# A decoder layer on one core: four edits at the two ends of its attention phase

## The reference, cut to what matters

```python
x = _layernorm(x + attn(x))        # 16 heads of 64, causal, softmax, output projection
x = _layernorm(x + xattn(x, ctx))  # 16 heads of 16, mask by key, biases
x = _layernorm(x + ffn(x))         # two groups of 32 experts, the best 2 of each

def _moe_group(x2, router_w, wg, wu, wd, top_k):
    scores = softmax(x2 @ router_w)
    expert_weights, expert_indices = top_k(scores, 2)
    # tokens sorted by expert, then per expert:
    ys = (silu(xs @ wg[e]) * (xs @ wu[e])) @ wd[e]
    return zeros_like(x2).at[tok].add(ys * weight)
out = (out0 * 2 + out1 * 2) / 4
```

## Time and profile before

| | us |
|---|---|
| median of 3 runs | 4497.11 |
| lowest, highest run | 4495.11, 4508.62 |
| the profiled execution, whole time | 4491.85 |
| its span, first to last instruction | 4490.1 |
| TensorE busy | 4356.7 (97%) |
| VectorE busy | 3698.2 (82%) |
| ScalarE busy | 3259.8 (73%) |
| GpSimd busy | 2742.9 (61%) |

### The profile page before, as it was taken

The page is one execution under the profiler, slowest core; times in us unless marked ns, Lnnn a source line. Parts: engine busy times, 40 slices in busy tenths (PEclk is TensorE's granted clock), DMA queues, the critical chain, the costliest instruction groups (busy, mean ns, idle before and its releaser), DMA issues. The chain is left out here.

```text
span 4490.1 us, 137989 instructions
## 1 busy us (share of the span) xinstructions
PE 4356.7 (97%) x42944; PEld 3811.3 (85%) x42944; DVE 3698.2 (82%) x18057; ACT 3259.8 (73%) x12741; POOL 2742.9 (61%) x3747
## 2 busy tenths in 40 slices
PE   7999999999999999999999999999995999999998
PEld 6988888888888888888888888888883778878886
DVE  4888888888888888888888888888886466658888
ACT  5888888888888888888888888888883444444444
POOL 3466666666666666666656666666566555557777
PEclk9999999999999999999999999999997999999999
DMA  5122121211221212112112111222215699988999
GB/s 170 48 71 67 67 69 65 66 65 63 73 67 65 69 65 66 65 64 73 66 66 68 65 66 65 66 71 67 68 60 162 203 342 342 318 279 284 310 307 290
DMA packets 477453, 552.60 MB, mean 123 GB/s; under 512 B 55632, under 2 KB 408144, under 8 KB 476240
## 3 DMA queue, kind: packets, MB, share of 16 engines
q1 hardware_dynamic: 350800, 296.21, 20.6%
q0 software_dynamic: 52224, 146.87, 8.7%
q10 hardware_dynamic: 73728, 100.70, 7.4%
HBM read 266.21 MB, written 277.35 MB: 121 GB/s over the span
## 5 line engine op out<-in xcount | busy, mean ns | idle before, releaser
L898 ACT ACTIVATE prob<-prob,negmax 128x128 f32<-128x128 f32 x2048 | 796.7, 391 | 299.4 <-DVE negmax L1032 299.4
L898 ACT ACTIVATE xprob<-xprob,xnegmax 128x128 f32<-128x128 f32 x2048 | 798.9, 400 | 3.8 <-DVE xnegmax L1032 3.8
L1364 POOL DMA_INDIRECT y_d<-y,to x576 | 563.6, 979 | 357.6 <-DVE y L1506 332.3
L1032 DVE CUSTOM_DVE_ANT_0 prob<-bank,causal 128x128 f32<-128x128 f32 x2048 | 452.8, 285 | 273.9 <-PE bank L787 248.8
L634 POOL DMA_INDIRECT xs_d<-xrow,place x512 | 554.9, 1084 | 133.4 <-issue 131.7
L1417 PE MATMUL bank<-moe,xgT 128*128 x2304 | 595.9, 382 | 2.6 <-issue 2.4
L597 POOL TENSOR_TENSOR rs<-spread_v,minus_half 128x1 f32<-128x1 f32 x256 | 146.7, 573 | 635.0 <-DVE spread_v L1106 634.8
L1080 DVE TENSOR_TENSOR xprob<-xprob,xinv 128x512 f32<-128x512 f32 x512 | 489.6, 956 | 17.5
L580 POOL CAST yTh<-yT 128x512 fp32r<-128x512 f32 x256 | 205.6, 803 | 431.9 <-ACT yT L934 431.9
L685 PE MATMUL bank<-xT0h,wqkv 128*128 128x256 f32 x2048 | 438.7, 298 | 19.4 <-DVE wqkv L434 11.3
L1032 DVE CUSTOM_DVE_ANT_0 xprob<-bank,xmask 128x128 f32<-128x128 f32 x2048 | 451.1, 284 | 0.3 <-PE bank L787 0.3
(11 more groups left out here) (174 smaller groups left out, 13330.7 us busy)
## 6 DMA issues: line engine op xcount, KB each, us to landing
xg<-xs_d SPq DMA_DIRECT2D x576, 129.0 KB
xs_d<-blank SPq DMA_DIRECT2D x248, 272.0 KB
rows<-y_d ACTq DMA_DIRECT2D x256, 256.0 KB
xT_s<-xT SPq DMA_DIRECT2D x128, 128.0 KB, 2.6
cT<-cT SPq DMA_DIRECT2D x128, 128.0 KB, 2.1
x_s<-x SPq DMA_DIRECT2D x128, 128.0 KB
x_d<-x SPq DMA_DIRECT2D x128, 128.0 KB, 1.9
sums<-x_d ACTq DMA_DIRECT2D x128, 128.0 KB
```

The source lines that it names most:

```text
L898: last = nc.scalar.activation(dst[:, h, :], dst[:, h, :], ACT.Exp, bias=src_bias[:, h:h + 1], scale=-1.0, accum_out=acc[:, h:h + 1])
L1032: last = nc.vector.tensor_tensor_reduce(dst[:, h, :], heads(h), bias[:, :], -1.0, float("inf"), ALU.add, ALU.min, least[:, h:h + 1])
L1364: nc.gpsimd.indirect_dma_start(y_d[:, :], bass.IndirectOffsetOnAxis(ap=to[:, m % NTO:m % NTO + 1].bitcast(U32), axis=0), y_s[q][:, :], Non ...
```

## The change

There are four edits.

1. ScalarE makes only the high part of weight 1 ahead of its steps. Those of weights 2 and 3 are made at the end of its steps n = -4 and n = -3, each behind two bank copies.
2. In GpSimd's even step `open_blocks` stands ahead of `scatter(b, (0, 1))`, not behind it.
3. The wait for landed scatters moves from GpSimd to SP, which then issues the two owner loads inside the attention block. The tile `owners` gets its own place behind the expert weights (the same addresses as before), and the second block's SP program begins with `xg`.
4. In VectorE's odd step the x2T copy stands ahead of the cross normalisation of the previous step's second half.

```diff
                     for p in (0, 1):
                         sp.wait_ge(x2_out[p], 16 * (NB // 2))
+                    for p in (0, 1):
+                        sp.wait_ge(placed[p], PLACED * (NB // 2))
+                    for g in range(NGRP):
+                        sp.dma_start(owners[:, g * TILES:(g + 1) * TILES, :],
+                                     xs_d[g].rearrange("(n p) d -> p n d", p=P)[0:1, :, CODE:OWNER + 1]).then_inc(owners_in, 16)
...
+                        b = due(n, 12, NB)
+                        if b is not None:
+                            open_blocks(b)
                         b = due(n, 14, NB)
                         if b is not None:
                             scatter(b, (0, 1))
-                        b = due(n, 12, NB)
-                        if b is not None:
-                            open_blocks(b)
...
                     steps_of(double_step)
-                    for p in (0, 1):
-                        pool.wait_ge(placed[p], PLACED * (NB // 2))
...
                 def _(act):
-                    for n in (1, 2, 3):
-                        weight_high(nc.scalar.copy, act, n)
+                    weight_high(nc.scalar.copy, act, 1)
                     act.wait_ge(weights_in, W_IN)
...
                             owners(n)
+                        if n in (FROM, FROM + 1):
+                            weight_high(nc.scalar.copy, act, n - FROM + 2)
...
                         masked(n)
                         cross_masked(n)
+                        move_transposed(n, "x2t")
                         cross_normalise(n - 1, 1)
-                        move_transposed(n, "x2t")
                         normalise(n, 0)
...
                 def _(sp):
-                    for g in range(NGRP):
-                        sp.dma_start(owners[:, g * TILES:(g + 1) * TILES, :],
-                                     xs_d[g].rearrange("(n p) d -> p n d", p=P)[0:1, :, CODE:OWNER + 1]).then_inc(owners_in, 16)
-
                     def iteration(t, n):
```

More of the change, by code:

```diff
@@ L205, in decoder_layer @@
         moe_cols = moe[:, :, :].rearrange("p e n -> p (e n)")
+        owners = nc.alloc_sbuf_tensor_at("owners", [1, NT, 2], F32, offset=moe_at + PLACES * WCOL * 4)
+        owners_in = sem("owners_in")
         moe_in = sem("moe_in")
@@ L1257, in decoder_layer @@
             STEPS = NT + E
+            assert nc.sbuf_base == moe_at + PLACES * WCOL * 4
             rows = sb("rows", [P, NR, TOPK, D])
@@ L1261, in decoder_layer @@
             flat = rows[0:1, :, :, :].rearrange("p r j d -> p (r j d)")
-            owners = flat[:, 0:2 * NT].rearrange("p (n c) -> p n c", c=2)
             wraps = flat[:, 2 * NT:2 * NT + TILES]
@@ L1278, in decoder_layer @@
             XB, GB, HB, YB = banks[0:2], banks[2:4], banks[4], banks[5:7]
-            owners_in, tabs_ready, pack_step, spare_ready, to_made = (
-                sem(n) for n in ("owners_in", "tabs_ready", "pack_step", "spare_ready", "to_made"))
+            tabs_ready, pack_step, spare_ready, to_made = (
+                sem(n) for n in ("tabs_ready", "pack_step", "spare_ready", "to_made"))
             xg_in = [sem(f"xg_in{q}") for q in range(NX)]
```

## The result

Four runs of the changed kernel on one chip have a median of 4457.53 us (4450.22 to 4461.27), four runs of the kernel before beside them 4496.11 us. The ratio is 0.9907, 95% interval [0.9888, 0.9925]: 0.9% faster. The forecast was 4469 (4459 to 4482). The profiled execution of the changed kernel took 4455.09 us (span 4453.3), so the two profiled executions lie 36.8 us apart. Most of that lies neither at the start nor at the end of the attention phase, which the title names: edits 2 and 4 act in every pair of steps.

A forecast was written before the change was run, and what follows sets the result against it. TensorE was taken to bound the attention stretch. Terms 8.5 + 13.4 + 2.1 + 0 + 4.2 = 28.2 us took the profiled 4491.85 to 4463.7, stated as 4469 against the median of 4497.11; range 4459 to 4482.

The forecast's parts named there:

- The start: Weight preparation: emptying banks between weight parts starts the v job earlier; 8.5 us, bounds 6.0 and 9.0.
- The copy moved forward: VectorE's odd step: x2T copy 0.81 us earlier removes TensorE's 61 router waits; 13.4 us, bounds 8 and 14.
- rival A: Steady part gives nothing: VectorE, late by its own work, holds TensorE at the next scores instead; 4482, chance 0.12.
- The two signs: Attention stretch: row "router waits for x2T" gone or under 2 us, and TensorE idle under 3 us.
- Blocks ahead of scatters: GpSimd's even step: eight block operations (2.8 us) pass two scatters (2.7 us), nothing added; value 0.
- rival B: Even step: more collisions delay the root for x2, making VectorE late at the masks; slower, 4531, chance 0.03.
- the root comes at the same time but for collisions: GpSimd's even step: block operations and scatters both precede the root for x2, so swapping them gains 0.
- the sum stays: GpSimd's even step: a scatter beside self normalisations loses at most what block operations gain by leaving; value 0.
- only its own 13.35 us of idle time can be won there: Attention stretch, 100 to 3300 us: TensorE, busy 3186.65 of 3200 us, bounds it, capping the gain at its idle time.
- The last batches: Last steps: the moved x2T copy shortens the same router wait, 7.3 us in 4 pieces; 2.1 us, bounds 0 and 3.5.
- The hand-over: Attention to experts: SP loads owners before the barrier; 3.35 us plus 0.8 from GpSimd's earlier drain, 4.2, bounds 2.8 and 5.2.
- C: Start gives nothing: bank copies wait for something landing near 22 us, v job stays at 36.80; 4477, chance 0.06.

## Why the prediction was right in direction and short in size

- **The start: right.** 8.8 us measured, 8.7 worked out and 8.5 taken. Bank copies at 15.41 and 16.91, TensorE on at 17.56, v job at 27.99. The copies came a little earlier than the 16.5 expected. The pace did not fall back to the cold one: the granted clock is 1.00 (2.4 GHz) in each window between 14 and 24 us.
- **The copy moved forward: the step that failed first.** "TensorE has no other wait in the stretch, so its end comes 13.4 us earlier" took the one row of waits for the one cause. The copy alone gave 4.7 us, and rival A's mechanism, at a chance of 0.12, is what happened to it, though not at the scores but with 59 waits at the rank job's bank. That no other wait was in the list meant only that this one came first. The two signs that the prediction named, the router's row gone and TensorE idle under 3 us, are both there, and they don't speak for its cause: the copy alone takes the row away and leaves 11.4 us. That the steady part gained by at least what was forecast is luck.
- **Blocks ahead of scatters, "Value 0": wrong, and the largest term.** It is worth 23.1 us alone and 20.0 behind edit 4. The prediction had both facts in hand, the 1.69 us of the earlier trace rows as the reason for VectorE's lateness, and "the block operations move beside masks" against rival B. It used them against a loss and never asked for the gain. The step that failed is "the root comes at the same time but for collisions": the collisions were the whole of it, and the root comes 0.77 us earlier in the batches that waited. By the port rule it quoted from the Trainium skill ("SBUF — State Buffer", Who interferes with whom: whoever starts first holds the pair for the whole instruction) an order on GpSimd matters through who starts first. The trace agrees, with 0.69 against 1.69 us for the same operation. The page's warning on scatters, which the prediction used too, is for VectorE's copies in a two-port mode, not for these normalisations; the two scatters that moved beside them take 1.09 and 0.97 in the rows above, as little as elsewhere. The sentence "the sum stays" counted only the scatters' losses. Rival B had the right place and the wrong sign: the chain from stretched work on GpSimd over a late root to a late VectorE was at work in the kernel before, and edit 2 ended it.
- **The two errors offset each other in part.** 13.4 + 0 was said, 24.7 measured. 11.3 of the miss lie here, the rest of the terms take a part of it back (0.3 + 1.3 - 2.6 - 0.3 - 1.0 - 0.6 = -2.9), which leaves 8.4 of the 8.6 between 4463.7 and 4455.09. That puts the time out of the range.
- **The size of the wait was mis-sized too.** 13.4 us by ends of matmuls, 23.3 by starts. So "only its own 13.35 us of idle time can be won there" was no bound. Had the cause been right, the term would still have been 10 us short.
- **The last batches: wrong, 2.1 forecast, -0.5 measured.** Edit 4 alone gives nothing there (router 118 to 127: 194.67, before 194.23). Which wait takes the place of each of the four pieces of the earlier trace rows was not followed.
- **The hand-over: right in mechanism, low in size.** 5.5 against 4.2. The half that was taken for the drain is a whole: the drain ends 1.7 us earlier (5.3 us behind the last scatter's issue in place of 7.0), and the barrier comes with it (0.8 had been counted). The other part is 3.8, where 3.35 had been taken for waiting on xg; TensorE starts 2.9 us behind the barrier, not 3.3, since the table (2.78 from the start of packing) and not xg comes last.
- **Rivals.** The prediction's C (the start gives nothing) was wrong. Its B had a condition, a root that comes later; it came earlier, by 0.77 us, since the block operations and a scatter before it were no longer stretched.

Three things stay open. Why the normalisations meet the subtraction in every second batch and not in all was not tested; in that half the root starts 1.38 us later (-2.08 for -3.46), behind a step that ends with the split of xT and a cast stretched to 1.07 (0.61 in the other half), and no run takes the split away. What each single collision is worth in TensorE's time was not separated. And what makes the expert stretch vary by 12 us is not known.

## What to carry to other kernels

A row of waits names where a late engine is first met, not why it is late; before pricing its removal, look at the late engine for instructions that take longer than their like, and ask which order on its neighbour would end that. Two engines that collide share a phase: a shift of a few tenths decides who starts first, so a small delay can cost little (7 us for 0.33) and a larger one all of it (85 us for 0.73). Less busy time of an engine is no gain by itself: some 80 us less on VectorE gave 23 us in one kernel and nothing in another. Take the length of a TensorE wait from start to start of neighbouring matmuls, since the idle time shown here was under two thirds of it (13.4 of 23.3, 18.6 of 31.7).

## What the runs showed of the hardware

- A 128x512 two-input operation on VectorE takes 0.69 us alone, 1.02 us when it starts 0.12 behind a GpSimd cast, and 1.6 to 1.8 when it starts behind a GpSimd two-input subtraction of 1.28; a 128x64 one took 1.24 in place of 0.22 there. The other way round, 128x64 operations on GpSimd took 0.77 in place of 0.30 beside a self normalisation of VectorE. Where VectorE starts first, GpSimd's cast takes 0.96 in place of 0.61.
- GpSimd's drain at the end of the block ended 5.3 us behind the end of the last scatter's issue where it was entered ahead of that (3431.53 to 3443.64, issue done at 3438.34), and 5.30 us behind its own start where it was entered after the scatters had landed (before, and with the wait on GpSimd).
